# A decoder layer's mixer with the scan's decay factors in PSUM, shared attention banks, gate projections a batch ahead, and no engine loop

## What is computed

```
# 1. mixer (Mamba-like), DI = 512 channels, 16 states, 4 conv taps
x_ssm, res = split(norm(x) @ W_in.T)
x_ssm = silu(conv(x_ssm) + b_conv)
dt    = softplus(x_ssm @ W_dt.T + b_dt);  A = -exp(A_log);  B = x_ssm @ W_x.T (second half)
h_t   = exp(dt_t * A) * h_(t-1) + dt_t * B_t * x_t          # per channel and state
y_t   = sum over states of h_t + D * x_t
x    += (y * silu(res)) @ W_out.T
# 2. cross attention, one head of 256, context of 1601 rows with a mask
x    += softmax(where(mask, -1e9, Q K^T)) V @ Wo.T + bo
# 3. routed network, 8 experts of width 704, two chosen for each token
x    += sum over the two experts of score * (silu(x W1) * (x W2)) W3
```

## Time and profile before

| | us |
|---|---|
| median of 3 runs | 1309.44 (1306.83 to 1310.84) |
| span of the profiled execution | 1352.2 |
| head, up to the first scan | 54.1 |
| first batch, to the last scan's end | 54.1 to 226.5 |
| second, with the gap behind it | 226.5 to 441.1 |
| third | 441.1 to 649.4 |
| fourth | 649.4 to 845.7 |
| tail and routed network | 845.7 to 1352.2 |
| busy: PE, VectorE, ScalarE, GpSimd | 966.2, 945.3, 446.0, 728.5 |

### The profile page before, as it was taken

One profiled execution on the slowest core, in us unless ns is written; L12 is line 12 of the kernel. 1 busy time (PEld: TensorE's weight loads), 2 busy tenths in 40 slices (PEclk: granted clock), 3 DMA queues, 4 the chain that ended last, 5 costly groups with the idle time before them and its releaser, 6 DMA issues. The chain is left out here.

```text
span 1352.2 us, 15599 instructions
## 1 busy us (share of the span) xinstructions
PE 966.2 (71%) x4316; PEld 667.9 (49%) x4317; DVE 945.3 (70%) x1313; ACT 446.0 (33%) x823; POOL 728.5 (54%) x497
## 2 busy tenths in 40 slices
PE   3664554958875777885867886797365999999690
PEld 1222211525552434553434563476254999999580
DVE  4499999898998989899989799242721334344134
ACT  2343433424453334353343342022211222222120
POOL 2376667676556586556687665210274444544405
PEclk8776866979986788988688985898586999999795
DMA  9510002000006000005100003000462323211204
GB/s 325 203 32 0 0 32 93 0 7 7 1 32 216 2 0 12 0 0 204 47 0 13 1 0 126 0 13 16 150 224 59 103 95 103 95 39 39 78 28 128
DMA packets 48948, 85.30 MB, mean 63 GB/s; under 512 B 6292, under 2 KB 38696, under 8 KB 46856
## 3 DMA queue, kind: packets, MB, share of 16 engines
q1 hardware_dynamic: 43032, 65.77, 14.4%
q0 software_dynamic: 5872, 19.02, 4.7%
HBM read 65.64 MB, written 14.55 MB: 59 GB/s over the span
## 5 line engine op out<-in xcount | busy, mean ns | idle before, releaser
L404 POOL TENSOR_TENSOR u<-dtx,b_all 128x512 f32<-128x512 f32 x256 | 433.1, 1704 | 233.5 <-DVE h L655 230.8
L655 DVE TENSOR_TENSOR_SCAN h<-da,u 128x512 f32<-128x512 f32 x256 | 415.2, 1644 | 32.9 <-POOL u L404 20.6
L784 PE MATMUL ysum<-h,ident 128*128 128x512 f32 x256 | 186.0, 817 | 226.1 <-DVE h L642 185.5
L486 ACT ACTIVATE da<-dt_,a_neg 128x512 f32<-128x512 f32 x256 | 177.4, 717 | 142.1 <-DVE h L655 141.8
L784 PEld LDWEIGHTS ysum<-h,ident 128*128 128x128 f32 x256 | 50.6, 236 | 314.9 <-DVE h L642 273.0
L642 DVE TENSOR_TENSOR h<-h 128x512 f32<-128x512 f32 x128 | 168.0, 1313 | 0.0
L1373 DVE TENSOR_TENSOR hid<-act_,ps_u 128x352 f32<-128x352 f32 x78 | 40.5, 521 | 120.2 <-ACT act_ L1227 88.8
L924 PEld LDWEIGHTS pv<-pT,ctx_n 128*128 128x128 f32 (+1 forms) x832 | 106.9, 204 | 12.6 <-issue 9.2
L924 PE MATMUL pv<-pT,ctx_n 128*128 128x128 f32 (+1 forms) x832 | 109.5, 287 | 0.0
L895 PE MATMUL pa<-ctx_t,xnT_a 128*128 128x401 f32 (+1 forms) x256 | 107.4, 555 | 1.4 <-ACT xnT_a L531 1.4
L1509 PE MATMUL ps_y<-w_hi,hidT_hi 128*128 x234 | 71.6, 306 | 13.6 <-issue 10.9
(11 more groups left out here) (224 smaller groups left out, 1890.0 us busy)
## 6 DMA issues: line engine op xcount, KB each, us to landing
b_all<-b_dram SPq DMA_DIRECT2D x16, 1024.0 KB, 4.7
ctx_t<-in_ctxT SPq DMA_DIRECT2D x4, 1601.0 KB
ctx_n<-in_ctx SPq DMA_DIRECT2D x4, 1536.0 KB
ffn_sorted<-yg SPq DMA_DIRECT2D x1, 4992.0 KB, 22.4
ffn_sorted<-y_sb SPq DMA_DIRECT2D x39, 128.0 KB
tok_in<-tok SPq DMA_DIRECT2D x35, 128.0 KB
mask<-in_mask SPq DMA_DIRECT2D x16, 200.1 KB, 2.4
w_raw<-in_w1T SPq DMA_DIRECT2D x4, 704.0 KB
```

The lines of the kernel that those rows point to most:

```text
L404: nc.gpsimd.tensor_tensor(u[:, i % 2, :], dtx[:, j % 2, :], b_all[:, n, :], ALU.mult).then_inc(u_ok, 1)
L486: nc.scalar.activation(da[:, i % DS, :], dt_[:, j % 2, :], ACT.Exp, scale=a_neg[:, j, n:n + 1]).then_inc(da_ok, 1)
L655: nc.vector.tensor_tensor_scan(h[:, i % HS, :], da[:, i % DS, :], u[:, i % 2, :], 0.0, ALU.mult, ALU.add).then_inc(scan_ok, 1)
L784: nc.tensor.matmul(ysum[:], ident[:], h[:, 2 * p % HS, :], start=p % (NST // 2) == 0, stop=(p + 1) % (NST // 2) == 0).then_inc(sum_ok, 1)
```

## The change

- `da` moves from four SBUF buffers to two PSUM banks (`DS = 2`). ScalarE writes there, and the scan reads there.
- The banks for that come from the transposes: they now use `pa0` and `pa1` in turn with the scores, with waits on picks and copies. Row constants move to `pv`, and the output projection of attention goes to the second half of `pv`.
- The gate projections of batch b+1 move from body b+1 to body b, as do their SiLUs. `gate` gets eight rows in place of four; a copy takes the projection out of its bank (`res_copy`), and the SiLUs of convolution and gate run in one piece (`silus`).
- One table `AT` with other steps, and with the steps of each row tile written out, is used for all five bodies; `ALONE` is gone.
- The bodies of batches 1 and 2 are written out; addresses and semaphore values are constants, and the small extra instructions are gone.

```diff
+    "score": ((15, 16, 17, 18), (19, 20, 22, 23), (28, 29, 30, 31), (37, 38, 39, 40)),
+    "pick": ((17, 18, 19, 20), (21, 22, 24, 25), (30, 31, 32, 33), (39, 40, 41, 42)),
+    "fill": (15, 18, 28, 37), "max": (20, 25, 33, 42), "exp": (23, 28, 36, 45), "inverse": (26, 31, 39, 48),
+    "p_turn": ((24, 25, 26, 27), (32, 33, 34, 36), (41, 42, 43, 44), (46, 47, 48, 49)),
+    "p_copy": ((26, 27, 28, 29), (34, 35, 36, 38), (43, 44, 45, 46), (48, 49, 50, 51)),
+    "av": ((27, 28, 29, 30), (35, 36, 37, 39), (44, 45, 46, 47), (51, 52, 53, 54)),
+    "av_copy": (31, 41, 49, 55), "out": (32, 42, 49, 56), "x2": (34, 43, 51, 57),
...
+    "ln_m_stat": 11, "ln_m_root": 12, "ln_m_norm": 13, "ln_m_turn": 13, "ln_m_copy": 16,
+    "in_proj": (17, 22, 24, 27), "tap": (19, 24, 27, 30), "conv": (20, 25, 28, 31),
+    "res_proj": (30, 33, 37, 39), "res_copy": (32, 35, 40, 42), "silu": 44,
+    "b_proj": 46, "b_copy": 49,
+    "dt_proj": (52, 5, 18, 34), "softplus": (56, 9, 21, 37), "dt_add": (57, 10, 22, 38), "dtx": (59, 12, 24, 40),
...
-    DS = 4
+    DS = 2
...
-        gate = sb("gate", [P, KI, S])
+        gate = sb("gate", [P, 2 * KI, S])
...
-        da = sb("da", [P, DS, S])
...
-        pt = [ps("pt0"), ps("pt1")]
         pv = ps("pv")
-        RES_BANKS = (pm[0], pm[1], pt[1], pv)
-        CONV_BANKS = (pm[0], pm[1], pm[1], pm[0])
-        DT_BANKS = (pm[0], pt[0], pm[0], pm[0])
+        da = [ps("da0"), ps("da1")]
+        CONV_BANKS = (pm[1], pm[0], pm[1], pm[0])
+        RES_BANKS = (pm[1], pm[0], pm[0], pm[1])
+        DT_BANKS = (pm[1], pv, pm[0], pm[1])
...
-                with pool.Fori(1, B - 1) as b:
+                for b in range(1, B - 1):
...
-                def silu_conv(m):
+                def silus(m):
                     act.wait_ge(conv_step, (TAPS - 1) * (m * KI + KI))
-                    nc.scalar.copy(act_scrap[:, KI:KI + 1], ident[:, 0:1])
                     for j in range(KI):
                         nc.scalar.activation(of_row(xs, m, j), of_row(xs, m, j), ACT.Silu).then_inc(silu_ok, 1)
+                    act.wait_ge(res_ev, m * KI + KI)
+                    for j in range(KI):
+                        nc.scalar.activation(of_row(gate, m, j), of_row(gate, m, j), ACT.Silu).then_inc(res_ok, 1)
                     exp_and_ln()
...
-                            nc.scalar.activation(da[:, i % DS, :], dt_[:, j % 2, :], ACT.Exp,
+                            nc.scalar.activation(da[i % DS][:], dt_[:, j % 2, :], ACT.Exp,
...
+                            for k in range(KI):
+                                if i == when["res_copy"][k]:
+                                    act.wait_ge(res_mm, m * KI + k + 1)
...
+                                    nc.scalar.copy(of_row(gate, m, k), RES_BANKS[k][:]).then_inc(res_ev, 1)
...
-                            nc.vector.tensor_tensor_scan(h[:, i % HS, :], da[:, i % DS, :], u[:, i % 2, :], 0.0,
+                            nc.vector.tensor_tensor_scan(h[:, i % HS, :], da[i % DS][:], u[:, i % 2, :], 0.0,
...
                             if g == 0:
                                 pe.wait_ge(exp_ok, a * T + q + 1)
...
+                            if g >= 2:
                                 pe.wait_ge(pt_ok, NPT * (a * T + q) + g - 1)
+                            elif q < T - 1:
+                                pe.wait_ge(pick_ok, QCH * (a * T + q + 1) + g + 3)
+                            else:
+                                pe.wait_ge(pt_ok, NPT * (a * T + q - 1) + g + 3)
...
+                            if q > 0 and g == 0:
+                                pe.wait_ge(x2_ok, a * T + q)
```

More of the change, by code:

```diff
@@ L81 @@
[L81 to L103, removed]
@@ L388, in body @@
                 def body(b, scan, inp, att_):
-                    when = AT if scan else ALONE
+                    when = AT
                     a, m = b - 1, b + 1
@@ L533, in body @@
                             for q in range(T):
[L534 to L535 removed]
+                                if i == when["exp"][q]:
                                     act.wait_ge(nmax_ok, a * T + q + 1)
@@ L562, in _ @@
                 body(0, True, True, False)
-                with act.Fori(1, B - 1) as b:
+                for b in range(1, B - 1):
                     body(b, True, True, True)
@@ L688, in body @@
                                     convolve(m, k)
-                            if not scan and i == when["conv_silu"]:
+                            if not scan and i == when["silu"]:
                                 set_up_biases()
@@ L736, in _ @@
                 body(0, True, True, False)
-                with dve.Fori(1, B - 1) as b:
+                for b in range(1, B - 1):
                     body(b, True, True, True)
@@ L904, in attention @@
+                        if i in when["av"][q]:
+                            g = when["av"][q].index(i)
+                            if q > 0 and g == 0:
+                                pe.wait_ge(x2_ok, a * T + q)
                             elif g == 0:
                                 pe.wait_ge(c_ok, a + 1)
[L906 to L911 removed]
@@ L965, in _ @@
                 body(0, True, True, False)
-                with pe.Fori(1, B - 1) as b:
+                for b in range(1, B - 1):
                     body(b, True, True, True)
```

182 lines of the change are left out of this document (77 added, 105 removed).

## The result

The changed kernel takes 1232.92 us (median of 6 runs, 1231.13 to 1241.34) against 1310.59 us for the kernel before in the same comparison: ratio 0.9425, interval 0.9394 to 0.9456. It is 77.7 us faster, where 151 were forecast. The time lies inside the range of 1125 to 1235, 2 us from its upper end, and 4 us from the 1229 of the second rival.

The account below looks back on a forecast made before the run. VectorE was taken as the bound, stretched by waiting for GpSimd. Batches 135 + 2 x 175 + 149 = 634 us against 791.6 save 157.6; less 3 head, 4 tail: 150.6. 1309.4 - 150.6 = 1158.8, about 1160 us; range 1125 to 1235.

Parts of the forecast that it names:

- rival 2: Batches: PE and ScalarE become the bound, full batches 198, last 168, first 140; 1229 us in all; chance 0.22.
- The lock: VectorE instructions with two SBUF inputs and GpSimd wait for each other, about 1.04 us; a scan reading PSUM would not.
- rival 3: Scans: the waiting between VectorE and GpSimd stays, by operand position or GpSimd's own reading; 1326 us; chance 0.05.
- Rhythm and price of a PSUM operand: Scan loop: two steps take 3.27 us instead of 4.93; a PSUM operand adds 0.08 us per scan, 20 us over 256.
- VectorE's other work, head: VectorE beyond scans and pair sums: 46 us a full batch, 20 first, 31 last; head before the scan 3 us longer.
- Tail: Attention of the last batch alone, 100 us before: shared banks make PE wait, 4 us more (0 to 10).
- Banks, order, gates ahead: Full batches: between VectorE's sum, 160, and PE's with waits, 191, the middle 175 is taken; last 149, first 135.
- the upper sum: Full batch on PE: 156.0 busy plus waits of 10.4 for y, 19.5 for pair sums, about 5 elsewhere: 191 us.
- two decay buffers: ScalarE's factors, one scan of cover instead of three: stalls of 9 us a batch preparing the next, 3 the last.
- rival 4: ScalarE's list: with one-scan factor cover, its waits for PE or row maxima stop the scan; slower, 1324 us; chance 0.05.
- The sign that was named: VectorE idle behind factors for more than 25 us a batch would show the prediction wrong (rival 2 and rival 4).
- Rival 5: Everything overlaps: full batches 160, last 142, first 131, gain 191.6 before head and tail; 1125 us; chance 0.08.

Follow-up runs that it names:

- depth four by turns: The changed kernel with four decay buffers, in turn a PSUM bank and an SBUF buffer, gate rows six instead of eight; ratio 0.9741.

## Why the prediction was wrong

**The lock: right.** Both sides of it: scans no longer stretch, and u is at most 1722 ns. The Trainium skill's rule ("SBUF — State Buffer", "Who interferes with whom"), that a VectorE instruction with at most one SBUF input does not contend with GpSimd, holds as written, not by operand position: 256 of 256 scans stay between 1189 and 1225 ns, and rival 3 is out. With the pair sums later in both, PSUM is worth 799.6 - 654.5 = 145 us of batches. (Pair sums were said to spread to twice their shortest; the earlier trace rows has three times, 658 to 2030 ns. It changes nothing.)

**Rhythm and price of a PSUM operand: too long.** The chain is the one forecast: the pair sum holds u up, and the second scan waits for this u. It takes 3.03 us and not 3.27, 31 us less over the 128 rhythms. A third of it, 0.08, is the price of the PSUM operand: the median scan is 1.216 us, as with SBUF alone. The price stands in the rhythm once, so it is worth 10 us there and not 20. The rest is that a scan was put in by its length and not by the 1.13 us to the next start, and that u begins while the pair sum still runs.

**VectorE's other work, head: right** (118, 149, 149, 135; the first scan at 56.3 us instead of 54.1, forecast 57). **Tail**: 107 us for 100, forecast 104. **Routed network**: the two waits of the earlier trace rows are missing from the trace of the changed kernel, so it was right to count from the median of the runs.

**The failed step** is the one of "Banks, order, gates ahead" where a full batch was put between VectorE's sum, 160, and PE's sum with its waits, 191, and the prediction says "I take the middle, 175". The batches are 197 and 196. PE's sum was nearly the right size: busy 156.6 for the 156.0, waits for pairs 19.4 for the 19.5, for y 5.8 for 10.4, others 13.7 for 5. That it came so near is in part luck: no row gave the half by which the waits for pairs were cut, and the errors of the other two terms nearly cancel. The last batch stood at 149 for 174.5, the first at 135 for 144.1, in the same way. No row spoke for the middle; what led to it was the sentence held against rival 2, that PE's waits for VectorE grow short by themselves once VectorE is faster. They went from 49.3 to 25.2 us, which the upper sum already had, and no further: PE takes its list in order, and a pair sum stands in it right behind a scan that PE itself may have held up through ScalarE or GpSimd. The later pair sums show that the place in the list matters: the same work takes 184.8 and 184.6 us, where 175 were forecast; 127.8 for 135; 157.3 for 149. They do not show that the waits alone did it, since PE's idle time in the full batches stayed at 39 us and its busy time fell.

The account of the miss, in batches: 711.2 measured, 634 forecast, 77 more. 707.2 - 654.5 = 53 of it goes with the place of the pair sums, 4 is the scatter between two runs of the changed kernel (711.2 and 707.2). The other 20.5 are stalls that remain: the third batch then has 184.6 - 149.2 = 35.4 us of idle VectorE, where the term "two decay buffers" had 9 and the lean to PE 15.

**Two decay buffers.** The size of the SiLU stall was fair: 3.8 us behind the SiLUs and 1.5 at the next scan, for 6. But the term counted only ScalarE's own long work. What stands in ScalarE's list in front of factors and waits for PE (L513, L520, L422) was left to rival 4 as harmless, being waits of an engine that runs ahead; with a cover of one factor it no longer runs ahead, and a single such wait stopped the scan for 8.11 us. The sign that was named, more than 25 us behind factors in a batch, came true by a hair: 26.7 in the second and 26.1 in the third.

**Rivals.** Rival 2 (1229, chance 0.22) is what happened, with full batches of 197 for its 198, the first 144 for 140, the last 174 for 168. Its name is half right: PE and ScalarE became the bound together, by waiting for each other; ScalarE is busy only 85 of 196 us. That depth alone is at fault (rival 4) is not shown: depth two costs nothing in the old order, where VectorE is full, and depth four by turns gives back 25 of 93 us, with half of the lock in the way. Four factor buffers all in PSUM were not run. Rival 5 takes head and tail off twice: its gain of 191.6 already has their 7 us, so its time is 1118 and not 1125.

**Open.** Why, with the lock and with later pair sums, the new order, with its banks and two buffers, is still 18 us longer than the old one (799.6 against 781.3); how much of the 53 us came through PE's clock; and what the routed network waits for in some comparisons.

## What to carry to other kernels

When the full engine is made faster, add up for the next one its busy time and those of its waits that its list forces on it, and take that sum as the new length, until a change of order says how these waits go away; taking a value between the two engines' sums is a forecast that somebody will reorder the list. (All of its waits would be too many: with them any engine's sum is the old length.) Then look for rings: an engine that stands right after it has made others stand. The cheap cure is to put its consuming instruction a few steps later in its in-order list wherever the buffers allow, which cost nothing here and gave 57 us, more than twice what leaving out 96 of 208 value products of each attention gave. Afterwards compare the engine's busy time as well as its waits, for here much of the gain stands in the busy time. The same edit is worth nothing while another engine is full, so it must be tried again after each large gain.

## What the runs showed of the hardware

- A scan with its first operand in PSUM takes what it takes from SBUF: 1189 to 1225 ns against the 1190 of the shortest before. By the fixed cycles of the Trainium skill ("VectorE: DVE Perf Modes", "The TRN2 errata"), 120 from PSUM and 58 from SBUF, an estimate is 0.065 us more. The runs do not show it (median 1216 ns, for 1226 before), and the measurement decides.
- PE's busy time is no fixed amount of work: 573 matmuls of a full batch took 156.6 us in the one order and 145.7 in the other, at a mean granted clock of 0.86 and 0.90. Two pair-sum matmuls took 2.07 us where the granted clock was 0.50, and 1.02 us where it was 0.99.
- The routed network, which no edit touches, takes 361 to 366 us in some comparisons and 402 to 408 in others, on the same chips, with 31 to 52 us of waits for "another core or an unknown queue" in the chain of the second kind only. The batches do not follow it: the kernel before with its loop written out has 207.7 and 207.2 us in its full batches (second kind), with later pair sums 207.5 and 207.5 (first kind).
